# A sparse-expert transformer layer on one Trainium2 core: GpSimd's queue sends of the last two sequences, one in every second expert step

## What is computed

```
x = layernorm(x + attention(x))           # 16 heads of 64, causal
x = layernorm(x + ffn(x))

def ffn(x):
    xn = normalised x * gamma + beta
    probs = softmax(router(xn) / 1.5)     # 8 experts
    w, idx = top_k(probs, 2)
    return x + sum over the two chosen experts of  w * (silu(xn @ W1[e]) @ W2[e])
```

## Time and profile before

| what | us |
|---|---|
| median of 3 runs | 1299.85 |
| lowest and highest run | 1299.53, 1302.07 |
| span of the profiled execution | 1337.7 |
| TensorE busy in the span | 1284.4 |
| GpSimd busy in the span | 750.5 |

### The profile page before, as it was taken

The page is one execution under the profiler, slowest core; times in us unless marked ns, Lnnn a source line. Parts: engine busy times, 40 slices in busy tenths (PEclk is TensorE's granted clock), DMA queues, the critical chain, the costliest instruction groups (busy, mean ns, idle before and its releaser), DMA issues.

```text
span 1337.7 us, 36549 instructions
## 1 busy us (share of the span) xinstructions
PE 1284.4 (96%) x11106; PEld 1132.1 (85%) x11106; DVE 1096.5 (82%) x5167; ACT 1163.3 (87%) x3655; POOL 750.5 (56%) x1333
## 2 busy tenths in 40 slices
PE   6999999999999999999999999999987899999997
PEld 6888888888888888888888888888866789988883
DVE  7888888888888888888888888888974677777756
ACT  7999999999888999898988989988875789999947
POOL 2346666566556566655655656665565555545545
PEclk9999999999999999999999999999998999999999
DMA  5000001000000000000000000000321222222228
GB/s 204 6 13 22 22 23 38 24 22 14 14 14 14 14 14 14 18 22 14 14 14 14 14 13 14 15 16 22 142 89 46 69 69 74 72 68 70 58 77 330
DMA packets 49216, 60.99 MB, mean 46 GB/s; under 512 B 8304, under 2 KB 35059, under 8 KB 48768
## 3 DMA queue, kind: packets, MB, share of 16 engines
q1 hardware_dynamic: 39376, 41.44, 9.6%
q0 software_dynamic: 8640, 17.13, 3.8%
q10 hardware_dynamic: 1008, 0.08, 0.1%
HBM read 30.72 MB, written 28.81 MB: 45 GB/s over the span
## 4 chain that ended last, share of the span: by engine, by line
PE 79%; ACT 10%; issue 3%; another core or an unknown queue 2%; DVE 1%; ACTq 1%; DMA 1%; POOL 1%; SPq 0%; POOLq 0%; DVEq 0%
PE ps_a L1259 14%; PE ps_s L1302 12%; PE ps_s L1281 11%; PE ps_f L1337 7%; PE ps_b L1294 7%; PE ps_f L1294 6%; PE ps_s L1284 4%; PE ps_b L1259 4%; PE ps_f L1259 3%; PE ps_s L1259 3%; ACT f_y L798 2%; ACT weights L813 2%; PE ps_s L1618 2%; ACT f_y L788 2%
## 5 line engine op out<-in xcount | busy, mean ns | idle before, releaser
L678 ACT ACTIVATE f_y<-f_y,neg_max 128x256 f32<-128x256 f32 x512 | 256.2, 500 | 46.9 <-DVE neg_max L960 43.7
L960 DVE CUSTOM_DVE_ANT_0 f_y<-ps_s,mask 128x256 f32<-128x256 f32 x512 | 214.4, 419 | 61.0 <-PE ps_s L1284 60.7
L1259 PE MATMUL ps_a<-xt_hi,weights 128*128 128x256 f32 x1024 | 240.3, 298 | 0.0
L577 POOL TENSOR_TENSOR ot_lo<-f_y,ot_hi 128x512 fp32r<-128x512 f32 x128 | 165.1, 1290 | 115.6 <-PE ps_s L1284 110.3
L643 POOL DMA_INDIRECT y_tok<-f_y,m_dest x142 | 140.6, 990 | 128.4 <-DVE m_dest L1165 97.2
L976 DVE TENSOR_SCALAR f_y<-f_y,inv_sums 128x256 f32<-128x256 f32 x512 | 196.5, 384 | 7.0
L681 ACT ACTIVATE f_y<-f_y,neg_max 128x128 f32<-128x128 f32 x512 | 199.7, 390 | 0.0
L1302 PE MATMUL ps_s<-ident,f_y 128*128 128x128 f32 x1536 | 195.5, 273 | 0.2 <-DVE neg_max L964 0.2
L1259 PEld LDWEIGHTS ps_a<-xt_hi,weights 128*128 128x128 f32 x1024 | 174.6, 188 | 16.0 <-issue 10.8
L1281 PE MATMUL ps_s<-qk 64*128 64x256 f32 x1024 | 176.4, 421 | 6.7 <-ACT pt L726 3.6
L1302 PEld LDWEIGHTS ps_s<-ident,f_y 128*128 128x128 f32 x1536 | 171.4, 141 | 5.3 <-DVE neg_max L964 0.6
(11 more groups left out here) (227 smaller groups left out, 3482.7 us busy)
## 6 DMA issues: line engine op xcount, KB each, us to landing
m_x<-queue SPq DMA_DIRECT2D x71, 133.0 KB
f_y<-y_tok SPq DMA_DIRECT2D x32, 256.0 KB, 6.8
queue<-empty SPq DMA_DIRECT2D x8, 532.0 KB
x_raw<-in_x SPq DMA_DIRECT2D x32, 128.0 KB
out_x<-f_y SPq DMA_DIRECT2D x16, 256.0 KB, 6.1
y_tok<-f_y,m_dest POOLq DMA_INDIRECT x142
f_y<-in_w SPq DMA_DIRECT2D x1, 2048.0 KB, 11.2
m_w<-in_w SPq DMA_DIRECT2D x1, 2048.0 KB, 15.1
```

The lines of the kernel that those rows point to most:

```text
L577: pool.tensor_tensor(ot_lo[:, first:first + 2, :], ot[:, s % 2], ot_hi[:, first:first + 2, :].bitcast(F32), ALU.subtract).then_inc(ot_lo_d ...
L678: act.activation(row[:, 0:2 * P], row[:, 0:2 * P], ACT.Exp, scale=-1.0, bias=neg_max[:, pair, h, 0:1], accum_out=sums[:, d % 2, pair, h, 0:1])
L960: dve.tensor_tensor_reduce(out=row[:, 0:2 * P], in0=ps_s[:, pair, h, 0:2 * P], in1=mask[:].rearrange("p a b -> p (a b)"), scale=-1.0, scal ...
L1259: ins = pe.matmul(dst, lhs, rhs, start=(i == 0), stop=(i == len(terms) - 1))
```

## The change

On GpSimd only. The four queue sends of sequence 30 no longer go ahead of the loop over the steps: its slots come behind the row sends of step 0, and its sends go one each into steps 2, 4, 6 and 8, ahead of those steps' row sends. The slots of sequence 31 move from step 9 to step 11, and its sends go one each into steps 13, 15, 17 and 19.

```
-            def send_tokens(n, i):
-                par = n % 2
-                if i == 0:
+            def send_choice(n, i, k):
+                par, col = n % 2, i * TOP + k
+                if col == 0:
                     pool.wait_ge(slots_done, n - 1)
                     pool.wait_ge(keep_done, n - 1)
                     if n == SEQS - 1:
                         pool.wait_ge(tails_zeroed, 16 * E)
+                pool.indirect_dma_start(
+                    queue, bass.IndirectOffsetOnAxis(ap=slot_now[:, par, col:col + 1], axis=0),
+                    z[:, par, i, :], None).then_inc(tokens_sent[par], 16)
+
+            def send_tokens(n, i):
                 for k in range(TOP):
-                    col = i * TOP + k
-                    pool.indirect_dma_start(
-                        queue, bass.IndirectOffsetOnAxis(ap=slot_now[:, par, col:col + 1], axis=0),
-                        z[:, par, i, :], None).then_inc(tokens_sent[par], 16)
+                    send_choice(n, i, k)
...
             norm(SEQS)
-            slots(SEQS)
-            for i in range(TILES):
-                send_tokens(SEQS, i)
...
             for j in range(NJ):
                 if LATER <= j + 2 < NJ:
                     rest_of_expert_weights(j + 2)
-                if j == 9:
+                if j in (2, 4, 6, 8):
+                    send_choice(SEQS, (j // 2 - 1) // TOP, (j // 2 - 1) % TOP)
+                if j == 11:
                     slots(SEQS + 1)
-                    for i in range(TILES):
-                        send_tokens(SEQS + 1, i)
+                if j in (13, 15, 17, 19):
+                    send_choice(SEQS + 1, (j - 13) // 2 // TOP, (j - 13) // 2 % TOP)
                 pool.wait_ge(m_dest_done, j + 1)
                 pool.wait_ge(m_rows_done, j + 1)
                 for i in range(BLOCKS):
...
                     ).then_inc(m_y_sent[j % YBUFS], 16)
+                if j == 0:
+                    slots(SEQS)
```

## The result

The changed kernel takes 1303.49 us (median of 16 runs, 1301.62 to 1306.16), the kernel before 1299.66 in the runs beside them (16 runs, 1298.42 to 1303.39): ratio 1.0028, 95% interval 1.0021 to 1.0035. It is slower by 3.8 us. The forecast was 1298.85 with a range of 1292 to 1302.

What follows compares the result with a forecast made beforehand. The prediction took ScalarE to set the expert stage's pace at 3.49 us a step, with the late signals only in the profiled execution. Gains of 0.3 + 0.7 = 1.0 us gave 1298.85 against 1299.85, range 1292 to 1302.

Steps and rivals of the forecast that it cites:

- The step on the recorded execution: Expert stage: its 41.7 us excess belongs to the profiled execution, 37.85 us too long, leaving timed runs at most 3.9.
- late signals: Expert stage: TensorE's work is done but its signal reaches VectorE and ScalarE 6 to 8 us late.
- The signs named for the profile after: Expert stage: reordered sends, much smaller VectorE and ScalarE waits, clock above 0.90, span several to some 15 us shorter.
- Rival A: Expert stage: late signals also in timed runs, 18.7 us on offer; 1281 (chance 0.06) or near 1293.5 (0.22).
- The sum of the expert stage: Expert stage: gains of 0.3 + 0.7 = 1.0 us, with ends at 0 and 3.65.
- part 1: Step 0's row sends ahead of sequence 30's slots: landing 2.1 us late before, in time after; gain 0.3 us.
- part 3: Sequence 31's slots and sends moved later: step 9 lands 1.55 us late before, nothing late after; gain 0.7 us.
- Part 2: Sequence 30's queue sends in steps 2, 4, 6, 8: 1.29 us each, covered by spare time; price 0.
- rival B: Expert steps: queue sends at 2.9 us each hold up row sends behind them; about 5 us slower, 1304.5, chance 0.08.
- Part 4: Readers of the moved work: VectorE's gates and SyncE's row loads not delayed, instructions and bytes the same; price 0.

Runs made afterwards that it cites:

- e1: The kernel before, unchanged, run again for a second profile: 1299.96 us beside 1299.99 for the kernel before.
- e4: Kernel before with only sequence 31's part changed (slots in step 11, queue sends in steps 13, 15, 17, 19): 1305.3 us.
- First half alone: Kernel after with sequence 31 put back as before in step 9, so only sequence 30's part changed: 1298.86 us.
- the second comparison: Both kernels run again unchanged: the kernel after 1303.22 us beside 1299.99 for the kernel before.
- e6: Kernel after, but sequence 31's four queue sends together at step 19, its slots still in step 11: 1301.94 us.
- e10: Kernel after, but sequence 31's slots at step 9, first queue send right behind them, the others in steps 15, 17, 19: 1303.15 us.
- e11: Kernel after, but sequence 31's slots in step 13, right ahead of its first queue send, instead of step 11: 1303.05 us.
- e9: Kernel before, but in step 9 the two row sends come between sequence 31's slots and its four queue sends: 1299.89 us.

## Why the prediction was wrong

**The step on the recorded execution held.** "I take the late signals as belonging to the recorded execution": e1's record of the same kernel has none, and its span is 41.6 us shorter. Attention was no quicker there: the first of ScalarE's L788 in the expert stage begins at 988.71 us in e1 and at 989.27 in the first record. Why that one execution had the late signals is not shown; none of the later records has them. The signs named for the profile after (a shorter span, smaller waits, a clock above 0.90 from 994 to 1062) came, but e1 shows them too, with a clock of 1.00: they are not the change's doing. Rival A, with a chance of 0.28, was not there to be had.

**The sum of the expert stage held by luck, its split did not.** The forecast was 0.3 for part 1 and 0.7 for part 3. The chain of part 1 was right to a tenth (in e1 the rows of step 4 start at 1022.40, 0.08 us after the landing that 2.27 us give), but the 0.3 was mis-sized: ScalarE lost 1.6 us in that place, since most of VectorE's wait of 2.48 us was not absorbed. The 0.7 of part 3 was nothing. By the prediction step 9 lands at 1054.85, and VectorE wants its buffer for step 13 at 1053.3. In e1 the second row send of step 9 and VectorE's rows of step 13 are:

```profile
1050.67 1.08 POOL L643 DMA_INDIRECT y_tok<-f_y,m_dest  x1 [0.30 <-issue]
```

```profile
1055.28 0.61 DVE L1192 SCALAR_TENSOR_TENSOR f_y<-ps_a,m_gate,f_y 128x128 f32<-128x128 f32 x2
```

By the same 2.27 us step 9 lands at 1052.9, and VectorE comes for its buffer at 1055.28, without a wait: 2.3 us to spare instead of 1.55 late. e4 without its excess of DRAIN (1305.3 - 4.8) is no faster than the kernel before. First half alone: 1.1 us (interval 0 to 2.3). That this is near the predicted sum of 1.0 comes of two terms that missed in opposite directions.

**Part 2 held.** Queue sends take 0.96 us with a gap of 0.30, and no rows of VectorE wait for a send. So rival B came near the measured time (1304.5; its price of about 5 us on 1299.85 makes 1304.85) with a mechanism that didn't happen: the four of steps 13 to 19 took 0.96 us each. The Trainium skill's 3.1 us for a DMA that GpSimd issues beside a VectorE copy (SBUF — State Buffer, "A bandwidth-pool intuition that's wrong") is met by no send of the expert stage in these records: the longest took 1.25 us.

**Part 4 failed, and with it the forecast**: "Instructions and bytes stay the same ... Price 0". The sum has no term for the end of GpSimd's program. The instructions did stay the same, but the length of one of them, GpSimd's closing DRAIN, hangs on their order: 20 fewer row sends behind the last queue send (124 to 104), past the place of the fall, brought it from 1.64 to 8.83 us. The end of GpSimd's program was in the profile of before, 2.4 us ahead of SyncE, and the prediction read of the end only the last send and SyncE's loads. Nothing in that profile showed that the DRAIN could grow. What could be read there was how little of a cover it had. The balance: 1.5 us gained among the steps, 4.8 lost at the end, 3.3 by these rows; measured 3.8 and, in the second comparison, 3.2.

## What to carry to other kernels

Look at how every engine ends: the closing DRAINs in the profile and how far each is ahead of the engine that finishes last belong to a change's costs, above all on an engine whose sends are reordered. When a change does all that it was meant to in its stage and the time doesn't follow, compare the last 10 us of the two profiles first. A profiled execution 38 us longer than the timed runs is worth a second record before its waits are believed.

## What the runs showed of the hardware

- GpSimd's closing DRAIN took from 0.988 to 9.482 us, to 2 ns the same for the same number of row sends behind the last queue send, by 0.0817 us for each of them, with a fall of 8.82 us between 112 and 116. How the other queue sends are placed doesn't change it (e6, e10, e11: 8.828 to 8.830).
- A row send takes 0.971 us or 0.983 us for the rest of the kernel, after whether a row send or a queue send was the first behind the slots (e9 against e11). No time hangs on it here.
- One record of a kernel had ScalarE and VectorE idle for 5.6 to 7.6 us ahead of work that needs products of TensorE, which the profile has as done, and 268.5 us from step 5 to step 70; the next record of the same kernel had no such wait, and 229.75.
